# A pre-norm decoder layer on one core: layer norm by subtract and multiply, one transfer a shift row, other order tables

## What is computed

```python
x = x + self_attn(layernorm(x))            # causal, bias -slope_h * |i - j| (ALiBi)
x = x + cross_attn(layernorm(x), ctx)      # 120 context tokens
x = x + tanh(layernorm(x) @ W @ A1 @ A2 + bias)
layernorm(x) = (x - mean) / sqrt(var + 1e-5)
```

## Time and profile before

| | |
|---|---|
| runs | 2377.23, 2377.55, 2383.47 us, median 2377.55 |
| the profiled execution | 2373.22 us, its span 2371.5 us |
| granted TensorE clock, mean | 0.984 |
| TensorE, VectorE, ScalarE, POOL busy | 94%, 72%, 60%, 30% |
| DMA, mean rate | 103 GB/s |

### The profile page before, as it was taken

One profiled execution on the slowest core, in us unless ns is written; L12 is line 12 of the kernel. 1 busy time (PEld: TensorE's weight loads), 2 busy tenths in 40 slices (PEclk: granted clock), 3 DMA queues, 4 the chain that ended last, 5 costly groups with the idle time before them and its releaser, 6 DMA issues.

```text
span 2371.5 us, 67224 instructions
## 1 busy us (share of the span) xinstructions
PE 2229.0 (94%) x22072; PEld 1848.5 (78%) x22072; DVE 1708.8 (72%) x3710; ACT 1416.2 (60%) x3066; POOL 719.2 (30%) x1372
## 2 busy tenths in 40 slices
...
GB/s 134 124 95 106 109 107 95 118 106 98 115 107 89 109 120 85 113 111 96 103 116 98 104 107 108 95 116 107 98 113 110 86 109 120 88 111 111 98 73 23
DMA packets 167370, 244.83 MB, mean 103 GB/s; under 512 B 22176, under 2 KB 90512, under 8 KB 164248
## 3 DMA queue, kind: packets, MB, share of 16 engines
...
...
## 4 chain that ended last, share of the span: by engine, by line
PE 75%; DVE 8%; issue 5%; POOL 4%; DMA 3%; ACT 2%; SPq 2%; DVEq 0%; POOLq 0%; ACTq 0%
PE ps_misc L555 14%; PE ps_misc L541 14%; PE ps_score L630 7%; PE ps_max L612 5%; PE ps_score L639 5%; PE ps_score L629 4%; PE ps_attend L654 4%; PE ps_misc L684 4%; DVE neg_max_s L975 4%; PE ps_max L600 3%; PE ps_misc L525 3%; PE ps_misc L699 3%; PE ps_attend L673 2%; DMA q_stack<-neg_max_t_s 2%; PE ps_misc L566 2%
## 5 line engine op out<-in xcount | busy, mean ns | idle before, releaser
L813 ACT ACTIVATE probs<-ps_score 128x384 f32<-128x384 f32 x1024 | 476.2, 495 | 145.7 <-PE ps_score L630 142.7
L975 DVE TENSOR_REDUCE neg_max_s<-ps_max 128x2 f32<-128x512 f32 (+1 forms) x768 | 479.2, 679 | 5.7 <-PE ps_max L594 4.5
L820 ACT ACTIVATE xprobs<-ps_score 120x512 f32<-120x512 f32 x512 | 292.5, 597 | 251.6 <-PE ps_score L639 213.5
L1113 POOL TENSOR_SCALAR ve_LN<-mv_LN 128x2 f32<-128x2 f32 x192 | 37.0, 193 | 1112.7 <-DVE mv_LN L997 1092.7
L983 DVE TENSOR_REDUCE neg_max_x<-ps_max 128x4 f32<-128x480 f32 x512 | 316.6, 650 | 21.3 <-PE ps_max L612 9.6
L630 PE MATMUL ps_score<-q_stack,k_stack 128*128 128x256 f32 x1024 | 321.6, 335 | 0.0
L629 PE MATMUL ps_score<-q_stack,k_stack 128*128 128x128 f32 x1024 | 292.6, 286 | 17.7 <-DMA q_stack<-neg_max_t_s 12.3
L629 PEld LDWEIGHTS ps_score<-q_stack,k_stack 128*128 128x128 f32 x1024 | 194.7, 190 | 62.9 <-DMA q_stack<-neg_max_t_s 29.3
L1141 POOL TENSOR_TENSOR res<-res,chain_n 128x512 f32<-128x512 f32 x64 | 81.6, 1275 | 410.2 <-ACT chain_n L858 410.2
L639 PE MATMUL ps_score<-xq_stack,xk_stack 128*120 128x256 f32 x1024 | 201.6, 309 | 4.4 <-DMA xq_stack<-neg_max_t_x 3.5
L600 PE MATMUL ps_max<-k_stack,q_stack 127*128 127x256 bf16 x1024 | 194.8, 281 | 4.5 <-DVE neg_max_s L975 0.7
...
## 6 DMA issues: line engine op xcount, KB each, us to landing
k_stack<-k_nat SPq DMA_DIRECT2D x192, 256.0 KB, 3.8
q_stack<-q_nat SPq DMA_DIRECT2D x192, 256.0 KB, 3.7
xq_stack<-q_nat SPq DMA_DIRECT2D x192, 256.0 KB, 3.7
xk_stack<-scr_xk SPq DMA_DIRECT2D x192, 128.0 KB, 2.7
x_in<-in_x SPq DMA_DIRECT2D x64, 256.0 KB, 2.7
...
out_y<-res SPq DMA_DIRECT2D x64, 256.0 KB, 2.2
...
```

The source lines that it names most:

```text
L813: act.activation(probs[:, h % 8, :], bank_of("SCORE", i, b, h)[:, P:4 * P], ACT.Exp)\
L820: act.activation(xprobs[0:C, at:at + 2, :], blocks(bank_of("XSCORE", i, b, u))[0:C], ACT.Exp).then_inc(sem("xprobs_ready"), 1)
L975: dve.tensor_reduce(o, ins, AX.X, ALU.max, negate=True).then_inc(sem("max_taken"), 1)
```

## The change

It has three parts.

1. **Layer norm.** mr and nmr are gone; L1127 becomes `(x - mean) * rstd`, one instruction for a block as before, with the mean read from the moments.
2. **Shift rows.** The maxima are kept as (head, block) in place of (block, head), so that the transposed tile has the row's order and one transfer of 32 x 128 numbers writes the whole shift row. The waits that counted 32 a shift row count 16.
3. **Order tables.** All are new. They start at another place of the cycle, and some steps stand elsewhere in it.

```diff
 ORDER = {
...
-        ("XMAX", -1, 3), ("XMAX", -1, 4), ("XMAX", -1, 5), ("SCORE", 0, 14), ("LN3_T", -2, 0),
...
+        ("LN3_T", -2, 0), ("ATTEND", 0, 2), ("XMAX", -1, 5), ("XMAX", -1, 6), ("XK", 0, 0),
...
-        neg_max = {n: sb(f"neg_max_{n}", [P, NB, H]) for n in ("s", "x")}
+        neg_max = {n: sb(f"neg_max_{n}", [P, H, NB]) for n in ("s", "x")}
...
-                    for qb in range(NB):
-                        sp.dma_start(dst_of(b)[SHIFT:SHIFT + 1, :, qb * P:(qb + 1) * P].bitcast(F32),
-                                     neg_max_t[which][qb * H:(qb + 1) * H, :])\
-                            .then_inc(sem(f"{which}_shift_stacked"), 16)
+                    sp.dma_start(dst_of(b)[SHIFT:SHIFT + 1, :, :].rearrange("r h t -> r (h t)").bitcast(F32),
+                                 neg_max_t[which][:, :]).then_inc(sem(f"{which}_shift_stacked"), 16)
...
-                    wait(pe, "s_shift_stacked", 32, i, b, 32)
+                    wait(pe, "s_shift_stacked", 16, i, b, 16)
...
-                    ins, o = blocks(bk, 4), neg_max["s"][:, 0, 4 * g:4 * g + 4]
+                    ins, o = blocks(bk, 4), neg_max["s"][:, 4 * g:4 * g + 4, 0]
...
-                    wait(pool, s, 4, i, b, 2)
-                    pool.tensor_tensor(mr[:, :].unsqueeze(2), mv[:, :, 0:1], rstd[:, :].unsqueeze(2), ALU.mult)\
-                        .then_inc(sem(s), 1)
-                    wait(pool, s, 4, i, b, 3)
-                    alone(pool)
-                    pool.tensor_scalar(nmr[:, :], mr[:, :], -1.0, 0.0, ALU.mult, ALU.add).then_inc(sem(s), 1)
-                    wait(pool, s, 4, i, b, 4)
+                    wait(pool, s, 2, i, b, 2)
                     free(i, b)
                     alone(pool)
                     for a in range(NB):
-                        last = pool.tensor_scalar(dst[:, a, :], src[b % 2][:, a, :], rstd[:, a:a + 1],
-                                                  nmr[:, a:a + 1], ALU.mult, ALU.add)
+                        last = pool.tensor_scalar(dst[:, a, :], src[b % 2][:, a, :], mv[:, a, 0:1],
+                                                  rstd[:, a:a + 1], ALU.subtract, ALU.mult)
```

More of the change, by code:

```diff
@@ L66 @@
     "SP": (
-        ("LOAD_X", 1, 0), ("MAX_STACK", 0, 0), ("XK_STACK", -1, 0), ("LOAD_CTX", 0, 0),
-        ("XQ_STACK", -1, 0), ("K_STACK", 1, 0), ("Q_STACK", 1, 0), ("XMAX_STACK", -1, 0),
-        ("STORE", -2, 0), ("XK_SAVE", 0, 0),
+        ("LOAD_CTX", 0, 0), ("XQ_STACK", -1, 0), ("K_STACK", 1, 0), ("Q_STACK", 1, 0),
+        ("XMAX_STACK", -1, 0), ("XK_SAVE", 0, 0), ("STORE", -2, 0), ("LOAD_X", 2, 0),
+        ("MAX_STACK", 1, 0), ("XK_STACK", 0, 0),
     ),
     "PE": (
-        ("SCORE", 0, 4), ("ATTEND", 0, 0), ("SCORE", 0, 5), ("XOUT_T", -2, 0), ("SCORE", 0, 6),
@@ L79 @@
[L79 to L84, removed]
@@ new lines @@
+        ("SCORE", 0, 6), ("XOUT_T", -2, 0), ("SCORE", 0, 7), ("K", 1, 0), ("SCORE", 0, 8),
+        ("SCORE", 0, 9), ("XOUT_PROJ", -2, 0), ("SCORE", 0, 10), ("Q", 1, 0), ("XMAX", -1, 0),
+        ("SCORE", 0, 11), ("SCORE", 0, 12), ("ATTEND", 0, 1), ("XMAX", -1, 1), ("XMAX", -1, 2),
+        ("SCORE", 0, 13), ("XMAX", -1, 3), ("CTX_T", 0, 0), ("SCORE", 0, 14), ("XMAX", -1, 4),
+        ("LN3_T", -2, 0), ("ATTEND", 0, 2), ("XMAX", -1, 5), ("XMAX", -1, 6), ("XK", 0, 0),
+        ("XMAX", -1, 7), ("SCORE", 0, 15), ("FFN", -2, 0), ("MAX", 1, 0), ("MAX", 1, 1),
```

68 lines of the change are left out of this document (35 added, 33 removed).

## The result

| | before | with the change |
|---|---|---|
| runs, median (lowest to highest) | 2377.57 us (2377.23 to 2383.47) | 2472.66 us (2470.02 to 2474.55) |
| the profiled execution: its span | 2371.5 us | 2471.0 us |
| mean granted clock | 0.984 | 0.981 |

The ratio is 1.0394, with a 95% interval of 1.0379 to 1.041: the changed kernel is 95 us slower, where 55 us less were forecast. The mean granted clock is 0.3% lower (0.981 against 0.984), far too little for 4%.

What follows compares the result with a forecast made beforehand. TensorE, busy 94% of the span, was taken as the bound, with holes to close. -0.58 and -0.27 us a sequence, times 62, plus -2 us drain, gave -55 us: 2322.5 us, range 2303 to 2351.

Steps and rivals of the forecast that it cites:

- The normalisation: POOL's layer norm: two small steps go, the last pair starts 0.67 us earlier, at 560 ns an instruction.
- the rival: POOL's pair at each LN's end, longer by x; at twice 560 ns the kernel is slower, 2385 us; chance 0.06.
- the drain's 2: End of the run: the pipeline drains through two LNs and two shift rows, 2 us saved in all.
- The slack of 0.75 us in the new place: LN3_T, moved earlier in TensorE's order: LN3 ready 0.75 us before TensorE takes it, counting the shorter LN.
- Both together, 0.58 us: MAX_T to SCORE 0: with shorter LN and one transfer, the shift row stays last and the hole shrinks 0.58 us.
- the later XMAX_T: Cross shift row: its transfer, 0.58 us shorter, pays for XMAX_T standing two steps of MAX later; worth 0.
- Alone it would give only 0.4: The single shift-row transfer without the shorter LN: SCORE 0 gains only 0.4 us, up to TensorE being ready.
- from SCORE 0 to XQ nothing moves: TensorE's stretch after SCORE 0: no change, since ScalarE's exponentials, 495 ns each, pace SCORE 2 and 3.
- Tables, -0.27 us: New order tables: changes at XOUT_T, K and the XMAX stretch sum to -0.27 us a sequence.
- The gain at XOUT_T: XOUT_T in TensorE's table: one more SCORE stands ahead of it while VectorE finishes XQ's low part, -0.22 us.
- The wait of 0.15 at K: K in TensorE's table: an exponential on ScalarE delays its input, so K newly waits, +0.15 us.
- The slack of 0.08: LN3_T in its earlier place: 0.08 us to spare after the POOL delivers LN3, before counting the shorter LN.

Runs made afterwards that it cites:

- the cheap form: The changed kernel with its normalisation as (x + (-mean)) * rstd, the mean negated in a small step ahead of the power: 2317.84 us.
- the old LN: The normalisation of before, four small steps and x * rstd + nmr; put back into the changed kernel, with new tables and single transfer: 2353.27 us.
- the short normalisation: (x + (-mean)) * rstd, mean negated ahead of the power; on the kernel before, alone 2371.39 us, with the new tables but two transfers 2348.99 us.

## Why the prediction was wrong, and what in it was right

**The step that failed is "The normalisation".** It took the new form at 560 ns, the row of the old form with the same shapes, and set the upper bound at the 0.70 us of the power. Measured are 1225 ns, outside the bound. The reasoning behind it, that both forms do two operations on each element, counts operations and not their kinds; and the power's 0.70 us is a time for 2 elements, so it bounds nothing at 256. Both ends of the bound were taken from the wrong rows. One term of the sum was mis-sized by a factor of 2.2, and with it the sign of the whole turned. The text had the rival, with its 0.06, and had its warning in a row, that operations aren't alike.

**The rival's own price was too low.** With x = 2 x (1.225 - 0.56) = 1.33 us its formula gives (x - 0.5) + (x - 0.75) = 1.41 us lost against 0.85 gained: 0.56 x 62 less the drain's 2 is 33 us slower, 2410. Measured is 2472.66. From the table, the changed kernel against the one with all three parts and the cheap form, by interval:
- LN2: MAX_T to XQ is 0.59 + 0.33 = 0.92 us longer; the formula has 0.83;
- LN3: Q to FFN is 1.00 longer; the formula has 0.58. The slack of 0.75 us in the new place isn't there;
- LN1: XQ to K is 0.45 longer; the formula has no term for it. LN1_T was left out of the account.

Together 2.32 us with the small gain at K, so 0.91 more than 1.41, times 62 = 56 us: nearly all of the 62 missing. The room was smaller still than this says: the cheap form has one small step more than the forecast's LN (the negated mean, 0.27 us), so from the first small step to the end of the pair the dear LN takes 3.63 us and the cheap one 2.56. Of these 1.07 us TensorE pays 0.92 at LN2 and 1.00 at LN3.

**Both together, 0.58 us: right in kind, 0.1 too large.** The order of events was right in the cheap form: the shift row stays last. The merged landing was 2.1 and not 1.85 us, which takes 0.25 off 0.58; MAX_T to SCORE 0 is 2.88 us, not 2.63. Another 0.12 was gained between FFN and MAX_T, at XSCORE 0, so that 0.47 of the 0.58 came. The forecast had the shorter transfer pay for the later XMAX_T there and put the two at 0 together. The direction was right; it is why the transfer is worth more with the new tables than at SCORE 0 alone. The Trainium skill's sum for a transfer ("DMA: Bandwidth & Descriptors", Anatomy of one DMA), given for the other issuing path, has 0.02 us for the 8 KB more. The rows here have 0.3 (1.8 and 2.1 us), so it doesn't describe this gather of 32 rows into one partition.

**"Alone it would give only 0.4": measured 0.12.** The first 0.33 came, but "from SCORE 0 to XQ nothing moves" is wrong with the old LN: XHEADS_OUT 1 waits for LN2's second half. The prediction looked at the steps up to SCORE 0 and not at the next one that uses LN2's bank.

**Tables, -0.27 us: -0.36 where LN is short, half of the forecast with the old LN.** With the short normalisation they take the kernel from 2371.39 to 2348.99, 22 us. XQ to K has a fourth score (0.23 to 0.31 us each) and is only 0.04 longer. The gain at XOUT_T came: it starts 0.36 us after the score ahead of it, where it was 0.54 (-0.18, forecast -0.22). The wait of 0.15 at K didn't: K starts 0.17 us after the matmul ahead of it, as before, and its input is ready 0.16 us earlier (means over 49 sequences). Q to FFN has one score less and was 0.09 shorter with the old LN, 0.38 with the short one, because LN3_T in its new place waits for the old LN (the 31 waits above). The slack of 0.08 there was in truth a lack.

**The sum.** With the cheap form the three parts give 2377.6 - 2317.84 = 60 us, where -55 us was forecast (2322.5 for 2317.84). That isn't to the prediction's credit: that kernel isn't the change, and the nearness is in part luck, since the transfer gave less than forecast (0.47 of 0.58 us) and the tables more (0.36 for 0.27). It does show that, with the price of the subtract taken out, most of the holes that the forecast named are those that close. No part gives its share alone: 4, 10.5 and 8 us alone are 23, and together 60. The short LN alone is hidden behind the shift row, the transfer alone behind LN2, the tables alone in part behind LN3.
